# A graph layer's slot table from one product per tile, sums of messages by halves, SiLU and tanh outputs

## The chip, the cores and the metric

One core of a Trainium2 chip. The metric is the time of one execution on the device in microseconds (us); three runs of the kernel before were timed. One more execution was recorded by the hardware profiler, and all rows come from it.

## What is computed

A graph layer over 100,000 nodes with 160 features (64 scalars s and 32 vectors v of three components) and 25,000 edges. Cut to what matters:

```
h = relu(layernorm(x))                                   # every node
w = relu(edge_feature @ W_fc1) @ W_fc2                   # every edge, 224 wide
xs, xv = (s @ W_nl0)[dst], (v @ W_nl1)[dst]              # gathered from h
tp = w0*xs, w3*dot(xv, sh1), w1*xs*sh1, w2*xv, w4*cross(xv, sh1)
agg = segment_sum(tp, src, num_segments=N) / 32
out_s = agg_s @ W_out_s + s @ W_skip0                    # 96 wide
out_v = agg_v @ W_out_v + v @ W_skip1
result = x + concat(silu(out_s[:, :64]), sigmoid(out_s[:, 64:96]) * out_v)
```

## The kernel before

The engines run separate programs that meet at semaphores; nothing is scheduled by a planner. The order on each engine is the order in which the code is written. Loops are unrolled to some depth and closed with a hardware loop. There are three stages.

**Table** (`edge_tiles`, L299). The 25,000 edges are 200 tiles of 125. The nodes are 98 macro tiles of 1,024; eight nodes per partition; a *bin* holds the edges of two of those eight columns (256 nodes), so there are 392 bins with 128 slots each (`CAP`, L53). The stage finds for every edge its slot in its bin and writes a table of which message lies in which slot. Per tile: DVE makes a one-hot of the bin (`bins_of`, L645 to L648, four tiles ahead); PE adds three triangular and full products into running counts (`count`, L1040, called in L1058 to L1065, with `tri_rest`, `ones_bf`, `tri_before`); DVE multiplies the one-hot with the counts and sums (L659), which is the edge's rank; ACT turns the rank into a one-hot of the slot times the tile's number by Abs and Relu (L899, and L892 for the tile before), POOL into a one-hot times the row's number (L496); PE adds both into `p_tile` and `p_row` two tiles later (`table`, L1045 to L1051). At the end PE closes the groups (L1073), ACT copies `p_row` (L908), DVE finds the highest count (L667) and combines both into `slots_i` (L671). If a count exceeds `CAP`, a second, slow form of the nodes stage runs; it is not taken with the reference's inputs.

Ahead of the stage DVE prepares constants (L584 to L643) and the statistics of the first two gathered groups (`stats_e`, L652, L653); behind it DVE prepares edge directions and scales weights (L844 to L860).

**Messages** (`round_e` of each engine; 50 groups of four tiles). POOL gathers node rows, DVE and ACT normalise them, PE turns and multiplies them, DVE forms the products, PE projects them, and SP stores `messages`, 200 numbers per edge with the node's place in column `LOCAL`. Row 0 of `messages` is an empty one. The change leaves this stage alone.

**Nodes** (`round_n` of each engine; 98 macro tiles i). SP loads x three tiles ahead and stores the result. POOL fetches 4 x 128 messages by `slots_i` (L529, `fetch`, two tiles ahead) and raises the variance to the power -1/2 (L535). DVE: the output product of the second half of tile i-1 (`gate`, L757), `shift_n` (L628), `norm_last` (L802), `residual` of i-1 (L772), statistics of i+2 (L610 to L624) with three of the four one-hots of i+1 in its gaps (`hot_n`, L752), `gate` of the first half of i. ACT: sigmoid of both halves (L985), six of the eight normalisations (L958), evacuation of the turned tiles (L965, L966), and the fourth one-hot by Abs and Relu (`distances` L972, `last_hot` L979). PE: transposes (L1176, L1177), the skip products (L1184, L1188) and the sums of the messages (`add`, L1199), in which a one-hot of 128 slots by 128 places multiplies the fetched messages; four products per half tile.

What waits for what around the change: POOL's power waits for DVE's last statistic (L624), DVE's shift for POOL's power, ACT's and DVE's normalisation for the shift, PE's transposes for both. POOL's `fetch` waits for PE's sums four tiles back. In the table stage the rank waits for PE's third count, and PE's next counts for the rank of the tile in front.

## Time and profile before

| what | us |
|---|---|
| timed runs, median (lowest to highest) | 1365.98 (1364.35 to 1367.78) |
| the profiled execution, its own time | 1356.92 |
| its span, first to last instruction | 1355.0 |
| mean granted TensorE clock | 0.984 of full speed |
| busy: PE, DVE, ACT, POOL | 1271.0, 1207.4, 1071.5, 1080.8 |

A row of the profile names the line, the engine, the operation and the tiles written and read. PE is TensorE's matmul, PEld its weight load, DVE VectorE, ACT ScalarE, POOL GpSimd, SP SyncE. The matmuls overlap, so their lengths are longer than the distance at which they start. An instruction's idle time is what its engine stood still ahead of it, with what ended that; "issue" is a wait for nothing that the profile shows. Neighbouring instructions of one group are merged into one row with a count.

### The profile page before, as it was taken

What the parts mean: (1) busy time and instruction counts of PE and PEld (TensorE: products, weight loads), DVE (VectorE), ACT (ScalarE), POOL (GpSimd) and SP (SyncE); (2) the same over time, 40 slices, a digit from 0 to 9 for tenths busy, and PEclk for the clock granted to TensorE, in tenths of its full rate; (3) what the DMA queues carried; (4) which work ended last, traced back from release to release, by engine and by line L of the source; (5) the groups of instructions that cost most, each with busy time, mean ns of one, the idle gap of its engine ahead of it and who ended that gap; (6) DMA issues with size and microseconds to landing.
All of it is one profiled execution on the core that took longest, in us unless ns stands there. A gap on an engine that the chain in (4) does not pass through costs nothing.

```text
span 1355.0 us, 35147 instructions
## 1 busy us (share of the span) xinstructions
PE 1271.0 (94%) x9057; PEld 1142.1 (84%) x9057; DVE 1207.4 (89%) x4348; ACT 1071.5 (79%) x2574; POOL 1080.8 (80%) x1054
## 2 busy tenths in 40 slices
PE   3999979999999999977999999999999999999997
PEld 2777758888888888867899999999999999998996
DVE  6999988888889888856899999999999999999996
ACT  3999977888888888846788788878888888787785
POOL 6999988888878778417788888888888888888883
PEclk9999998999999999988999999999999999999999
DMA  3000003444434444325787887878777787878774
GB/s 109 1 0 0 0 23 83 109 111 113 108 104 118 109 113 108 91 71 140 215 241 227 231 230 230 239 225 240 227 233 228 232 231 233 238 229 234 227 233 128
DMA packets 90918, 212.25 MB, mean 157 GB/s; under 512 B 15030, under 2 KB 56281, under 8 KB 90878
## 3 DMA queue, kind: packets, MB, share of 16 engines
q1 hardware_dynamic: 62462, 155.23, 37.1%
q0 software_dynamic: 28416, 56.56, 17.6%
q8 instruction: 16, 0.26, 0.1%
q14 instruction: 24, 0.20, 0.0%
HBM read 127.73 MB, written 84.00 MB: 156 GB/s over the span
## 4 chain that ended last, share of the span: by engine, by line
PE 50%; POOL 18%; issue 13%; DMA 8%; ACT 5%; DVE 3%; ACTq 0%; POOLq 0%; SPq 0%; DVEq 0%
POOL mg L529 17%; PE bank L1042 7%; DMA mg<-messages,slot_m 7%; PE bank L1105 5%; PE bank L1049 5%; PE bank L1199 5%; PE bank L1184 4%; PE bank L1158 4%; PE bank L1134 3%; PE bank L1122 3%; PE bank L1089 3%; PE bank L1118 2%; PE bank L1120 2%; ACT nn L958 2%; PE bank L1176 2%
## 5 line engine op out<-in xcount | busy, mean ns | idle before, releaser
L529 POOL DMA_INDIRECT mg<-messages,slot_m x392 | 444.8, 1135 | 121.4 <-issue 110.2
L958 ACT ACTIVATE nn<-xb,n_bias,n_rstd 128x160 f32<-128x160 f32 x588 | 300.6, 655 | 22.3 <-DVE n_bias L628 21.4
L1199 PE MATMUL bank<-mg,hot 128*128 128x192 f32 x1568 | 299.2, 334 | 11.6 <-DVE hot L752 11.6
L1184 PE MATMUL bank<-wsk_a,nt_a 128*128 128x160 f32 x1568 | 294.8, 311 | 4.0 <-DVE ob L765 3.0
L1199 PEld LDWEIGHTS bank<-mg,hot 128*128 128x128 f32 x1568 | 251.7, 191 | 11.8 <-DVE hot L752 11.8
L480 POOL DMA_INDIRECT xg<-x,dst_g x200 | 207.4, 1037 | 61.9 <-issue 56.6
L1184 PEld LDWEIGHTS bank<-wsk_a,nt_a 128*128 128x128 f32 x1568 | 226.4, 192 | 13.2 <-issue 9.0
L610 DVE BATCH_NORM_STATS2 n_stat<-xb 128x6 f32<-128x160 f32 x784 | 186.6, 310 | 4.0 <-DMA xb<-x 3.8
L535 POOL TENSOR_TENSOR n_rstd<-n_sum,neg_half 128x8 f32<-128x8 f32 x98 | 163.7, 1671 | 15.4 <-DVE n_sum L624 13.4
L496 POOL TENSOR_SCALAR slot_r<-iota_slot,rank,row_no 125x128 bf16<-125x128 f16 x200 | 160.0, 804 | 6.1 <-DVE rank L659 0.5
L1176 PE MATMUL bank<-ident,nn 128*128 128x128 f32 x784 | 136.0, 296 | 26.1 <-ACT nn L958 21.9
L1176 PEld LDWEIGHTS bank<-ident,nn 128*128 128x128 f32 x784 | 113.3, 207 | 50.1 <-ACT nn L958 43.7
L965 ACT ACTIVATE nt_a<-bank 128x512 f32<-128x512 f32 x196 | 115.7, 590 | 40.7 <-PE bank L1177 38.7
L772 DVE TENSOR_TENSOR ob<-ob,xb 128x1280 f32<-128x1280 f32 x98 | 145.5, 1484 | 0.1
L1188 PE MATMUL bank<-wsk_z,nt_z 128*128 128x64 f32 x784 | 130.1, 248 | 0.0
L1188 PEld LDWEIGHTS bank<-wsk_z,nt_z 128*128 128x128 f32 x784 | 128.5, 191 | 0.0
L882 ACT ACTIVATE hn<-xg,e_bias,e_rstd 125x160 f32<-125x160 f32 x200 | 108.9, 653 | 17.9 <-DVE e_bias L628 17.9
L659 DVE CUSTOM_DVE_ANT_0 rank_junk<-bin_hot,bank 125x392 bf16<-125x392 bf16 x200 | 112.3, 561 | 4.6 <-PE bank L1042 1.4
L918 ACT ACTIVATE tpt<-bank 128x375 f32<-128x375 f32 x200 | 99.5, 497 | 13.1 <-PE bank L1105 11.8
L985 ACT ACTIVATE sg<-bank 128x384 f32<-128x384 f32 x196 | 94.2, 481 | 18.8 <-PE bank L1199 17.3
L752 DVE TENSOR_SCALAR hot<-iota_local,mg 128x256 f32<-128x256 f32 x294 | 93.8, 348 | 16.6 <-DMA mg<-messages,slot_m 16.4
L972 ACT ACTIVATE off<-iota_local,mg 128x256 f32<-128x256 f32 x98 | 49.7, 507 | 74.1 <-DMA mg<-messages,slot_m 74.0
(147 smaller groups left out, 2976.7 us busy)
## 6 DMA issues: line engine op xcount, KB each, us to landing
xb<-x SPq DMA_DIRECT2D x97, 640.0 KB, 6.0
out_dram<-ob SPq DMA_DIRECT2D x97, 640.0 KB, 3.6
messages<-msg SPq DMA_DIRECT2D x50, 390.6 KB
mg<-messages,slot_m POOLq DMA_INDIRECT x392, 5.2
ef<-edge_feat_t SPq DMA_DIRECT2D x50, 125.0 KB, 6.0
xg<-x,dst_g POOLq DMA_INDIRECT x200
xb<-x SPq DMA_DIRECT2D x1, 420.0 KB
out_dram<-ob SPq DMA_DIRECT2D x1, 420.0 KB
```

What stands on the lines that cost most here:

```text
L480: pool.indirect_dma_start(xg[:, b, t, :], None, x[:, :], bass.IndirectOffsetOnAxis(ap=dst_g[:, b, t:t + 1], axis=0)).then_inc(e_x[b], 16)
L496: pool.tensor_scalar(slot_r[:, k % GE, :], iota_slot[0:ET, :], rank[:, k:k + 1], row_no[:, 0:1], ALU.is_equal, ALU.mult).then_inc(b_row, 1)
L529: pool.indirect_dma_start(mg[:, u, k, :], None, messages[:, :], bass.IndirectOffsetOnAxis(ap=slot_m[:, u, k:k + 1], axis=0)).then_inc(n.g[ ...
L535: pool.tensor_tensor(n_rstd[:, u, :], n_sum[:, u, 4, :], neg_half[:, :], ALU.pow).then_inc(n.pw, 1)
L610: last = dve.bn_stats(stat[:, t, :], rows[:, t, :])
L772: dve.tensor_tensor(ob[:, u, :, :], ob[:, u, :, :], xb[:, u, :, :], ALU.add).then_inc(n.res, 1)
L958: last = act.activation(nn[:, u % 2, h, :, g % 4], xb[:, u, g, :], ACT.Relu, bias=n_bias[:, u, g:g + 1], scale=n_rstd[:, u, g:g + 1])
L965: act.activation(nt_a[:, h, :], q_t[h], ACT.Relu)
L1176: pe.transpose(q_t[h][:, t * P:(t + 1) * P], nn[:, u % 2, h, 0:P, t], ident[:])
L1184: pe.matmul(z[:, t, 0:F], nt_a[:, h, t * P:(t + 1) * P], wsk_a[:], start=(t % 2 == 0), stop=False, skip_group_check=True)
L1188: pe.matmul(z[:, 2 * j:2 * j + 2, F:Z], nt_z[:, h, :], wsk_z[:, 2 * V * j:2 * V * j + 2 * V], start=False, stop=every, skip_group_check=True)
L1199: last = pe.matmul(q_z[h][:, t, 0:Z], hot[:, u % 2, g // 2, (g % 2) * P:(g % 2) * P + P], mg[:, u, g // 2, 0:Z], start=False, stop=True, s ...
```

## The change

The table is made by one product per tile. Its slots hold a running number of the message within a block of ten tiles (`row_no` is now 125 k + row, for k = 0 to 9) in one of two tables by turns; how many blocks came before the slot was filled is found by counting, at each block's end, which slots are still empty (`empty`). The bin is now one pair of node columns with 64 slots each (`CAP` 64 for 128 nodes); both counts are kept in one number, with weight 16 for the even and 2^-12 for the odd column, and POOL takes them apart for five tiles at a time. ACT makes the whole slot vector. The counts and tables are f16 instead of bf16. In the nodes stage the one-hot of a bin is 128 x 128, all four on DVE, and each sum is a product over 64 partitions. The output's scalars come from SiLU straight into `ob`, and the gates are tanh(z/2) + 1, with the half in the weights. What is left out is marked by "...": declarations, semaphores, the setup of constants and renamed tiles.

```diff
-    CAP = P
+    CAP = P // 2
+    BR, BLOCK, BATCH = 20, 10, 5
+    W_EVEN, W_ODD, SHARE, ROUND = 2.0 ** 4, 2.0 ** -12, 2.0 ** 16, 1.5 * 2.0 ** 23
+    assert NT % BR == 0 and BR == 2 * BLOCK and BLOCK * ET < 2048 and ET * NT < 2 ** 15
...
-p_tile = bank[1][:, 0:NB]
-p_row = bank[2][:, 0:NB]
+p_tab = [bank[1][:, 0:NB], bank[2][:, 0:NB]]
...
-    def tile_b(t, k):
-        wait(pool, b_tab, t - GE + 1)
-        pool.wait_ge(b_rank, t + 1)
-        pool.sem_inc(s_held, 1)
-        pool.tensor_scalar(slot_r[:, k % GE, :], iota_slot[0:ET, :], rank[:, k:k + 1], row_no[:, 0:1],
-                           ALU.is_equal, ALU.mult).then_inc(b_row, 1)
+    def tile_b(t, k, q):
+        if k % BATCH == BATCH - 1:
+            n, b, first = BR // BATCH * q + k // BATCH, k // BATCH % 2, k - BATCH + 1
+            tiles = bass.ds(t - BATCH + 1, BATCH)
+            ranks = rank[:, first:k + 1]
+            pool.wait_ge(b_rank, t + 1)
+            wait(pool, b_slot, t - BR + 1)
+            pool.tensor_tensor(both[:, b, :], ranks, unit[:, tiles], ALU.mult).then_inc(b_split, 1)
+            pool.tensor_tensor(share[:, b, :], ranks, unit_odd[:, tiles], ALU.mult).then_inc(b_share, 1)
+            pool.wait_ge(b_split, 4 * n + 1)
+            pool.tensor_tensor(evens[:, b, :], both[:, b, :], rounder[:], ALU.add).then_inc(b_split, 1)
+            pool.wait_ge(b_share, 2 * n + 1)
+            pool.tensor_tensor(share[:, b, :], share[:, b, :], first_slot[:, tiles], ALU.add).then_inc(b_share, 1)
+            pool.wait_ge(b_split, 4 * n + 2)
+            pool.tensor_tensor(evens[:, b, :], evens[:, b, :], rounder[:], ALU.subtract).then_inc(b_split, 1)
+            pool.wait_ge(b_split, 4 * n + 3)
+            pool.tensor_tensor(evens[:, b, :], evens[:, b, :], sign[:, tiles], ALU.mult).then_inc(b_split, 1)
+            pool.wait_ge(b_split, 4 * n + 4)
+            pool.wait_ge(b_share, 2 * n + 2)
+            pool.tensor_tensor(slot[:, first:k + 1], evens[:, b, :], share[:, b, :], ALU.add).then_inc(b_dec, 1)
+        if isinstance(t, int) and t == BLOCK:
+            scales(0, 0)
+        if isinstance(t, int) and t == BR - 1:
+            scales(1, 1)
     pool.wait_ge(b_const, 1)
-    scales(0, 0)
-    scales(1, 1)
     edge_tiles(pool, tile_b)
...
+    link(dve.tensor_scalar(weight[:], odd[:], W_ODD - W_EVEN, W_EVEN, ALU.mult, ALU.add))
...
-    dve.memset(most[:], 0.0)
-    dve.tensor_scalar(neg_tile[:], tile_no[:], -1.0, None, ALU.mult).then_inc(b_const, 1)
+    dve.memset(empty[:, 0, :], 0.0)
+    link(dve.memset(empty[:, 1, :], 0.5))
     def bins_of(t, k):
         wait(dve, b_tab, t - BR + 1)
-        dve.tensor_scalar(bin_hot[:, k, :], iota_bin[0:ET, :], bin_of[:, bass.ds(t, 1)], None,
-                          ALU.is_equal).then_inc(b_hot, 1)
+        dve.tensor_scalar(bin_hot[:, k, :], iota_bin[0:ET, :], bin_of[:, bass.ds(t, 1)],
+                          weight[:, bass.ds(t, 1)], ALU.is_equal, ALU.mult).then_inc(b_hot, 1)
     for t in range(4):
         bins_of(t, t)
-    stats_e(0, 0)
-    stats_e(1, 1)
-    shift_e(0, 0)
-    def tile_b(t, k):
+    dve.tensor_scalar(first_slot[:], odd[:], float(CAP), None, ALU.mult)
+    dve.memset(rounder[:], ROUND)
+    dve.tensor_scalar(unit[:], odd[:], 1.0 / W_ODD / W_EVEN - W_EVEN ** -2, W_EVEN ** -2, ALU.mult, ALU.add)
+    dve.tensor_scalar(unit_odd[:], odd[:], SHARE / W_ODD / W_EVEN, None, ALU.mult)
+    dve.tensor_scalar(sign[:], odd[:], -SHARE - 1.0, 1.0, ALU.mult, ALU.add)
+    dve.tensor_copy(row_no[:], row_i[:])
+    link(dve.tensor_copy(unit_of_slot[:], part_i[:]))
+    dve.tensor_scalar(neg_row[:], row_no[:], -1.0, None, ALU.mult).then_inc(b_const, 1)
+    link(dve.tensor_scalar(unit_of_slot[:], unit_of_slot[:], float(CAP), None, ALU.is_ge))
+    link(dve.tensor_scalar(unit_of_slot[:], unit_of_slot[:], 1.0 / W_ODD - 1.0 / W_EVEN, 1.0 / W_EVEN,
+                           ALU.mult, ALU.add))
+    link(dve.tensor_tensor(vec_sq[:], vec[:], vec[:], ALU.mult))
+    link(dve.tensor_tensor(vec_d2[:], vec_sq[:, :, 0], vec_sq[:, :, 1], ALU.add))
+    dve.tensor_tensor(vec_d2[:], vec_d2[:], vec_sq[:, :, 2], ALU.add).then_inc(s_tab, 1)
+    link(dve.tensor_scalar(tmp_a[:], src_i[:], 3, P - 1, ALU.logical_shift_right, ALU.bitwise_and))
+    dve.tensor_copy(place_of[:, :, 0], tmp_a[:])
+    dve.tensor_copy(place_of[:, :, 1], src_i[:])
+    def tile_b(t, k, q):
+        if k % BLOCK == 3 and not (isinstance(t, int) and t < BR):
+            m = 2 * q + k // BLOCK - 2
+            r = k // BLOCK % 2
+            dve.wait_ge(b_tab, t - 13)
+            dve.scalar_tensor_tensor(out=empty[:, r, :], in0=p_tab[r], scalar=0.0, in1=empty[:, r, :],
+                                     op0=ALU.is_equal, op1=ALU.add).then_inc(b_empty, 1)
         wait(dve, b_rank, t - 1)
+        wait(dve, b_dec, BR // BATCH * q + k // BATCH + 1 - BR // BATCH)
         dve.wait_ge(b_pre, t + 1)
         dve.tensor_tensor_reduce(out=rank_junk[:, k % 2, :], in0=bin_hot[:, k, :], in1=p_cnt[k % 2], scale=1.0,
                                  scalar=0.0, op0=ALU.mult, op1=ALU.add,
                                  accum_out=rank[:, k:k + 1]).then_inc(b_rank, 1)
         if tile_exists(t + 4):
             bins_of(t + 4, (k + 4) % BR)
+        if isinstance(t, int) and t == BATCH:
+            stats_e(0, 0)
+        if isinstance(t, int) and t == BLOCK + BATCH:
+            stats_e(1, 1)
+        if isinstance(t, int) and t == BR - 1:
+            shift_e(0, 0)
     edge_tiles(dve, tile_b)
     dve.wait_ge(b_end, 1)
-    dve.reduce_max(most[:], p_cnt[(NT - 1) % 2], AX_X).then_inc(b_most, 1)
-    dve.wait_ge(b_most, 1)
-    dve.tensor_copy(most_i[:], most[:])
+    total = p_cnt[(NT - 1) % 2]
+    link(dve.tensor_scalar(whole[:], total, 1.0 / W_EVEN, ROUND, ALU.mult, ALU.add))
+    link(dve.tensor_scalar(whole[:], whole[:], ROUND, None, ALU.subtract))
+    dve.reduce_max(most[:, 0:1], whole[:], AX_X)
+    link(dve.scalar_tensor_tensor(out=rest[:], in0=total, scalar=1.0 / W_EVEN, in1=whole[:],
+                                  op0=ALU.mult, op1=ALU.subtract))
+    dve.reduce_max(most[:, 1:2], rest[:], AX_X)
     dve.wait_ge(b_rows_sb, 1)
-    dve.scalar_tensor_tensor(out=slots_i[:], in0=p_tile, scalar=float(ET), in1=tab_row[:],
-                             op0=ALU.mult, op1=ALU.add).then_inc(b_fin, 1)
+    for r in range(2):
+        last = dve.scalar_tensor_tensor(out=empty[:, r, :], in0=p_tab[r], scalar=0.0, in1=empty[:, r, :],
+                                        op0=ALU.is_gt, op1=ALU.mult)
+    link(last)
+    dve.tensor_scalar(most[:, 2:3], most[:, 1:2], SHARE, None, ALU.mult)
+    for r in range(2):
+        last = dve.scalar_tensor_tensor(out=tab_row[:, r, :], in0=empty[:, r, :], scalar=2.0 * BLOCK * ET,
+                                        in1=tab_row[:, r, :], op0=ALU.mult, op1=ALU.add)
+    link(last)
+    dve.tensor_tensor(most[:, 3:4], most[:, 0:1], most[:, 2:3], ALU.max)
+    link(dve.tensor_tensor(empty[:, 0, :], tab_row[:, 0, :], tab_row[:, 1, :], ALU.add))
+    dve.tensor_copy(most_i[:], most[:, 3:4])
+    dve.tensor_scalar(slots_i[:], empty[:, 0, :], float(ET * NT), None, ALU.min).then_inc(b_fin, 1)
...
-        def hot_n(i, u, bins=range(BPM - 1)):
+        def hot_n(i, u, bins=range(BPM)):
...
-            dve.tensor_tensor(o[:, :, 0:S], z[:, :, 0:S], sg[:, h, :, 0:S], ALU.mult)
+            dve.tensor_scalar(sg[:, h, :, :], sg[:, h, :, :], 1.0, None, ALU.add).then_inc(n.one, 1)
+            dve.wait_ge(n.fs, 2 * i + h + 1)
+            dve.wait_ge(n.one, 2 * i + h + 1)
             dve.tensor_tensor(o[:, :, S:F].rearrange("p t (i k) -> p t i k", i=3),
                               z[:, :, SG:Z].rearrange("p t (i k) -> p t i k", i=3),
-                              sg[:, h, :, S:SG].unsqueeze(2).to_broadcast((P, 4, 3, V)),
+                              sg[:, h, :, :].unsqueeze(2).to_broadcast((P, 4, 3, V)),
                               ALU.mult).then_inc(n.mul, 1)
...
+    dve.tensor_scalar(wsk_a[:, SG:F], wsk_a[:, SG:F], 0.5, None, ALU.mult)
+    last = dve.tensor_scalar(wsk_z[:], wsk_z[:], 0.5, None, ALU.mult)
...
-    norm_e(0, 0, range(GE))
     act.wait_ge(b_const, 1)
-    def slots_of(t, k):
-        act.activation(slot_t[:, k % GE, :], off_slot[:, k % GE, :], ACT.Relu,
-                       bias=tile_no[:, bass.ds(t, 1)], scale=neg_tile[:, bass.ds(t, 1)]).then_inc(b_slot, 1)
-    def tile_b(t, k):
-        wait(act, b_tab, t - GE + 1)
-        wait(act, b_off, t)
-        act.wait_ge(b_rank, t + 1)
-        act.activation(off_slot[:, k % GE, :], iota_slot[0:ET, :], ACT.Abs, bias=rank[:, k:k + 1],
+    def tile_b(t, k, q):
+        act.wait_ge(b_dec, BR // BATCH * q + k // BATCH + 1)
+        act.activation(off_slot[:, k % 2, :], iota_slot[0:ET, :], ACT.Abs, bias=slot[:, k:k + 1],
                        scale=-1.0).then_inc(b_off, 1)
-        if tile_exists(t - 1):
-            slots_of(t - 1, (k - 1) % BR)
+        wait(act, b_tab, t - BLOCK + 1)
+        act.wait_ge(b_off, t + 1)
+        r = k % BLOCK
+        act.activation(slot_v[:, r, :], off_slot[:, k % 2, :], ACT.Relu, bias=row_no[:, r:r + 1],
+                       scale=neg_row[:, r:r + 1]).then_inc(b_slot, 1)
+        if isinstance(t, int) and t == BR - 1:
+            norm_e(0, 0, range(GE))
     edge_tiles(act, tile_b)
-    act.wait_ge(b_off, NT)
-    slots_of(NT - 1, (NT - 1) % BR)
     act.wait_ge(b_end, 1)
-    act.activation(tab_row[:], p_row, ACT.Copy).then_inc(b_rows_sb, 1)
+    for r in range(2):
+        last = act.activation(tab_row[:, r, :], p_tab[r], ACT.Copy, scale=unit_of_slot[:, 0:1])
+    last.then_inc(b_rows_sb, 1)
...
-        def distances(i, u):
-            act.wait_ge(n.g[u], earlier(i, u, U, 64) + 64)
-            wait(act, n.hot_a, i)
-            act.activation(off[:], iota_local[:], ACT.Abs, bias=mg[:, u, BPM - 1, LOCAL:LOCAL + 1],
-                           scale=-1.0).then_inc(n.off, 1)
-        def last_hot(i, u):
-            wait(act, n.z, 2 * (i - 2) + 2)
-            act.wait_ge(n.off, i + 1)
-            act.activation(hot[:, u % 2, BPM - 1, :], off[:], ACT.Relu, bias=ones[:, 0:1],
-                           scale=-1.0).then_inc(n.hot_a, 1)
-        def sigmoids(i, h):
+        def gates(i, u, h):
+            if h == 0:
+                wait(act, n.st[u], earlier(i, u, U, 16))
             act.wait_ge(n.z, 2 * i + h + 1)
             wait(act, n.mul, 2 * i + h - 1)
-            act.activation(sg[:, h, :, :], q_z[h][:, :, 0:SG], ACT.Sigmoid).then_inc(n.sg, 1)
+            act.activation(sg[:, h, :, :], q_z[h][:, :, S:SG], ACT.Tanh, scale=0.5).then_inc(n.sg, 1)
+            act.activation(ob[:, u, 4 * h:4 * h + 4, 0:S], q_z[h][:, :, 0:S], ACT.Silu).then_inc(n.fs, 1)
...
-                sigmoids(i - 1, 1)
+                gates(i - 1, (u + 3) % U, 1)
             evacuate(i, 1)
             if macro_exists(i + 1):
                 norm(i + 1, (u + 1) % U, 0)
-                if not every:
-                    distances(i + 1, (u + 1) % U)
-            sigmoids(i, 0)
+            gates(i, u, 0)
...
-    def table(t, k):
+    def table(t, k, q):
+        if k % BLOCK == 0:
+            wait(pe, b_empty, 2 * q + k // BLOCK - 1)
         pe.wait_ge(b_slot, t + 1)
-        pe.wait_ge(b_row, t + 1)
-        for o, slot in ((p_tile, slot_t), (p_row, slot_r)):
-            last = pe.matmul(o, slot[:, k % GE, :], bin_hot[:, k, :], start=False, stop=False,
-                             skip_group_check=True)
-        last.then_inc(b_tab, 1)
...
-        if tile_exists(t - 2):
-            table(t - 2, (k - 2) % BR)
+        if tile_exists(t - BLOCK):
+            table(t - BLOCK, (k - BLOCK) % BR, q if k >= BLOCK else q - 1)
     edge_tiles(pe, tile_b)
-    table(NT - 2, (NT - 2) % BR)
-    table(NT - 1, (NT - 1) % BR)
-    for o in (p_cnt[0], p_cnt[1], p_tile, p_row):
-        last = pe.matmul(o, zeros_bf[0:ET, 0:o.shape[0]], zeros_bf[0:ET, :], start=False, stop=True,
+    for t in range(NT - BLOCK, NT):
+        table(t, t % BR, t // BR)
...
-            if h == 0:
-                pe.wait_ge(n.hot, i + 1)
-            else:
-                pe.wait_ge(n.hot_a, i + 1)
-            for t in range(4):
-                g = 4 * h + t
-                last = pe.matmul(q_z[h][:, t, 0:Z], hot[:, u % 2, g // 2, (g % 2) * P:(g % 2) * P + P],
-                                 mg[:, u, g // 2, 0:Z], start=False, stop=True, skip_group_check=True)
+            pe.wait_ge(n.hot, i + 1)
+            for t in (0, 2, 1, 3):
+                slots = slice(CAP * (t // 2), CAP * (t // 2) + CAP)
+                pair = 2 * h + t % 2
+                last = pe.matmul(q_z[h][:, t, 0:Z], hot[slots, u % 2, pair, :], mg[slots, u, pair, 0:Z],
+                                 start=False, stop=True, skip_group_check=True)
             last.then_inc(n.z, 1)
```

## Rows read from the trace of the kernel before

**Rows 1.** Busy time by stage: us; PE, PEld, DVE, ACT, POOL; clock, DMA, GB/s.

```profile
608.00:1332.00 724.00, 688.98 (x4787) 656.37 (x4788) 672.46 (x2400) 582.44 (x1441) 603.82 (x488) 0.99 0.78 226
1332.00:1355.00 23.00, 13.09 (x94) 12.58 (x92) 10.66 (x20) 8.14 (x19) 1.42 (x1) 0.86 0.30 88
```

**Rows 2.** Groups by line, 40 to 160 us: busy us, mean ns, idle before.

```profile
L1042 PE MATMUL bank<-bin_hot,tri_before 125*125 125x392 bf16 x145 | 47.7, 329 | 0.0
```

**Rows 3.** Timeline of DVE and PE at the table's start: start us, us.

```profile
23.84 0.56 DVE L659 CUSTOM_DVE_ANT_0 rank_junk<-bin_hot,bank 125x392 bf16<-125x392 bf16 x1
...
24.32 0.32 DVE L647 TENSOR_SCALAR bin_hot<-iota_bin,bin_of 125x392 bf16<-125x392 f16 x1
...
24.55 0.56 PE L1042 MATMUL bank<-bin_hot,tri_rest 125*125 125x392 bf16 x1 [9.15 <-DVE rank L659]
24.55 0.56 DVE L659 CUSTOM_DVE_ANT_0 rank_junk<-bin_hot,bank 125x392 bf16<-125x392 bf16 x1
...
29.03 0.33 PE L1042 MATMUL bank<-bin_hot,tri_before 125*125 125x392 bf16 x1
...
29.16 0.36 DVE L647 TENSOR_SCALAR bin_hot<-iota_bin,bin_of 125x392 bf16<-125x392 f16 x1
...
29.50 0.56 DVE L659 CUSTOM_DVE_ANT_0 rank_junk<-bin_hot,bank 125x392 bf16<-125x392 bf16 x1
```

**Rows 4.** Timeline of one tile of the nodes stage, POOL and DVE.

```profile
990.47 1.68 POOL L535 TENSOR_TENSOR n_rstd<-n_sum,neg_half 128x8 f32<-128x8 f32 x1
...
993.01 1.49 DVE L772 TENSOR_TENSOR ob<-ob,xb 128x1280 f32<-128x1280 f32 x1
993.65 1.67 POOL L529 DMA_INDIRECT mg<-messages,slot_m  x1 [0.30 <-issue]
...
995.62 0.95 POOL L529 DMA_INDIRECT mg<-messages,slot_m  x1 [0.30 <-issue]
...
997.55 0.16 DVE L624 SCALAR_TENSOR_TENSOR n_sum<-n_sum 128x8 f32<-128x8 f32 x1
...
997.87 1.67 POOL L535 TENSOR_TENSOR n_rstd<-n_sum,neg_half 128x8 f32<-128x8 f32 x1
```

**Rows 5.** Waits of POOL from 608 us on: total us, times, longest.

```profile
POOL n_rstd L535 <- DVE n_sum L624: 7.5, 12, 1.3
```

**Rows 6.** Timeline of DVE ahead of the first rank.

```profile
22.02 1.00 DVE L610 BATCH_NORM_STATS2 e_stat<-xg 125x6 f32<-125x160 f32 x4 [5.29 <-DMA xg<-x,dst_g]
```

**Rows 7.** Groups by line, whole execution: busy us, mean ns, idle before.

```profile
L518 POOL TENSOR_TENSOR cr_a<-w4xv,hat 125x128 f32<-125x128 f32 x50 | 20.6, 411 | 0.0
...
L985 ACT ACT_TABLE_LOAD x1 | 1.3, 1283 | 0.0
...
L600 DVE TENSOR_TENSOR bin_of<-tmp_a,tmp_b 125x200 f32<-125x200 int32 x1 | 0.4, 368 | 0.0
```

**Rows 8.** Timeline of the joint between table and messages, ACT and DVE.

```profile
190.53 0.86 ACT L892 ACTIVATE slot_t<-off_slot,tile_no,neg_tile 125x128 bf16<-125x128 f32 x2
...
192.65 0.50 ACT L908 ACTIVATE tab_row<-bank 128x392 f32<-128x392 f32 x1 [1.26 <-PE bank L1073]
...
193.32 0.56 DVE L671 SCALAR_TENSOR_TENSOR slots_i<-bank,tab_row 128x392 int32<-128x392 f32 x1
...
200.25 1.94 ACT L882 ACTIVATE hn<-xg,e_bias,e_rstd 125x160 f32<-125x160 f32 x4 [3.45 <-DVE e_bias L628]
```

**Rows 9.** Timeline of ACT in the table stage.

```profile
31.02 0.40 ACT L899 ACTIVATE off_slot<-iota_slot,rank 125x128 f32<-125x128 f16 x1
31.33 0.48 ACT L892 ACTIVATE slot_t<-off_slot,tile_no,neg_tile 125x128 bf16<-125x128 f32 x1
31.71 0.39 ACT L899 ACTIVATE off_slot<-iota_slot,rank 125x128 f32<-125x128 f16 x1
```

**Rows 10.** Timeline of ACT at the first tile of the nodes stage.

```profile
615.22 0.51 ACT L972 ACTIVATE off<-iota_local,mg 128x256 f32<-128x256 f32 x1 [13.89 <-DMA mg<-messages,slot_m]
615.76 0.51 ACT L979 ACTIVATE hot<-off,ones 128x256 f32<-128x256 f32 x1
```

135 lines of the change are left out of this document (73 added, 62 removed).

## The prediction

> **What bounds the kernel now.** I read the busy time by stage first: table (24 to 192 us), messages (202 to 596), nodes (608 to 1332). In the nodes stage all four engines are over 80% busy [rows 1], so the share does not say which sets the pace, and I went on to the lines and the waits.
>
> Table stage: 145 tiles in 120 us, 0.83 us each, with five matmuls of 392 columns that start 0.166 us apart, so PE is full [rows 2]. DVE is close behind: rank at 23.84, its bin_hot at 24.32, the next rank at 24.55, that is 0.71 per tile while POOL is not yet making slot_r [rows 3].
>
> Nodes stage: POOL. One tile of 1,024 nodes runs from power to power, 990.47 to 997.87, 7.40 us [rows 4]: 1.68 for the power and 5.72 for four gathers with their issue. From 608 on POOL waits for another engine's n_sum only 12 times, 7.5 us in all [rows 5]. The second gather takes 1.67 us, the third 0.95, because the second meets the residual add on DVE (993.01 to 994.50) [rows 4]. DVE's own loop is almost as long: from the power's end (992.15) it runs shift, norm_last, residual, statistics and hot, and has the next variance at 997.71, 0.16 us ahead of the next power [rows 4]. That is where the 12 waits come from.
>
> **The change, part by part.** The sum is made against the profiled execution, 1356.92 us with a span of 1355.0; the median of the three timed runs is 1365.98, 9.06 higher, and my difference is added to that.
>
> Start of the table stage. Before, rank 0 waits for the second gather's statistics, which begin at 22.02 after 5.29 us of waiting [rows 6]. They now stand at tiles 5 and 15. From 7.04 on DVE has three casts (0.7 us), seven operations on 200 columns (0.25 to 0.37 each [rows 7] for the dearest; 2.1), two memsets of 392 columns (0.8), four bin_hot (0.9), eight small ones (1.5), the vec operations (1.7) and place_of (0.7): estimated by width, rank 0 at 16.0 for 23.84. Gain 7.8 us, between 6 and 9.
>
> Pace. PE falls to four matmuls, 0.66 us. The loop over two tiles is 0.71 (rank 23.84 to tri_rest 24.55) plus two starts of 0.166 plus 0.47 (tri_before 29.03 to rank 29.50) [rows 3], or 0.76 per tile. DVE gives 0.71 plus 0.05, a tenth of a pass over PSUM like slots_i's 0.56 [rows 8], if bin_hot keeps the 0.23 it has with POOL idle. ACT is the largest. It has the same two activations, but before, Relu worked on the tile before, so they overlapped: 0.31 from Abs to Relu, 0.38 from Relu to Abs [rows 9]. Now Relu waits for its own Abs. The trace has that form once: off, 0.51 long, then hot 0.54 after its start [rows 10]. With an Abs of 0.40 this makes 0.43 + 0.39 = 0.82 us per tile, what PE took before. The matmul taken away buys almost nothing; ACT is late next. PE and DVE run ahead until PE stands at the table of ten tiles back.
>
> End of ACT's work. Rank 4 ended at 28.40 (29.50 less two tiles, plus 0.56 [rows 3]), 4.6 us after rank 0, so the first batch is ranked at 20.6. POOL decodes it in seven operations on five columns; 128 columns take 0.41 us [rows 7], and by columns it is far less: estimate 2.0 us with its waits, between 1.0 and 3.5, below the 4.1 of a batch either way, so only the first shows. ACT starts at 22.6, loses 1.9 and 1.8 us to the two statistics on DVE and 1.7 to norm_e (four in 1.94 [rows 8]), and has the last slots at 22.6 + 5.4 + 199 x 0.82 + 0.9 = 192.1, for 191.39 before [rows 8]. The early start is used up by the batch delay and by statistics that used to lie in a wait.
>
> After the last table. From the last slots to the table's copy it is 1.26 us (191.39 to 192.65), now as before. Then slots_i was ready at 193.88 [rows 8]. Now ten passes over 392 columns stand there, most of them a chain on DVE: 0.59 for one that reads PSUM (0.56 and the wait of 0.03), 0.5 for one that doesn't, 0.42 where nothing waits. That is 5.6 us, so 199.0, 5.1 later, with ACT's two copies beside it. ACT's next norm at 200.25 waits for DVE [rows 8], which goes through its whole list first, so all of it counts, with 0.4 for the two scalings of wsk. **Table and joint: +5.5 us**, from +1 (ACT at 0.80) to +10 (at 0.84).
>
> Messages: not touched, only moved. PE at a low clock in a longer joint is covered by DVE's list.
>
> Nodes. Half-high sums on PE, hot of 4 x 128 for 3 x 256 on DVE, off and hot gone from ACT (0.51 each [rows 10]), two shorter activations for one, a product less and a short addition more on DVE: all beside POOL, whose list is the same. Without POOL's cover this would be worth up to 0.7 us per tile on DVE and 1.2 on PE. The residual starts 0.86 us after the power by DVE's own order, so the slow gather stays, and 7.40 with it. What is given is slack: the variance comes 0.3 us sooner. Of the 7.5 us of waits [rows 5] I take 3.5 as gone, with 0 and 7.5 as ends. In the tail (1332 to 1355) PE is busy for 13.09 us [rows 1], and 16 of its 50 starts per tile go to half their time at best, 2.1 us; I take 1.5, between 0 and 2.5. **Nodes: -5 us.**
>
> Sum: +5.5 - 5 = +0.5, so 1366.5 us.
>
> **Rivals.** (a) *Table switches, slower.* There is one ACT_TABLE_LOAD of 1283 ns at the first Sigmoid [rows 7] and none after it. If SiLU and tanh sat in different tables, each half tile would load twice: 5.1 us per tile onto ACT's 5.9 (582.44 over 98 tiles [rows 1]) less 0.7, so 10.3 against 7.4; 98 times that is 290 us, 1656. It decides as soon as ACT passes 7.4. Against it: Relu, Copy and Sigmoid alternate today without a load. Chance 0.03. The Trainium skill, ScalarE: Activation LUTs, "Table sets: the hidden batching unit", says that functions are loaded as named sets, lists tanh with sigmoid and does not place SiLU; by its 2.66 us for every switch the loss would be 10.6 us per tile. The trace agrees on the 1283 ns.
>
> (b) *DVE becomes the bound, slower.* bin_hot gets a second scalar and a multiplication. With POOL at work the next rank came 0.34 after it (29.16 to 29.50 [rows 3]), though PE may have held it. If it stays at 0.34, a tile is 0.48 + 0.34 + 0.05 = 0.87 on DVE; the point from which it decides is 0.82. The table ends 7 us later than in my sum: 1373.5. With 0.43, half the rate, it is 0.96 per tile and 1391. For it: this form is not in the trace. Against: the 0.23 without POOL. Chance 0.20, and 0.05 for ACT at 0.85 or more, at much the same price.
>
> (c) *ACT's wait costs nothing, faster.* With Relu 0.31 after its own Abs, DVE and the two-tile loop set 0.78, and ACT ends 8 us sooner: 1358.5. Against it stands the 0.54 after 0.51 [rows 10]. Chance 0.22.
>
> (d) *The second gather gets free of the residual, faster.* It would take 0.95 for 1.67 [rows 4], but DVE's loop then binds near 7.0: 94 tiles by 0.4, 38 us, 1329. Nothing moves the residual. Chance 0.05.
>
> The fallback, which repeats the nodes stage, would need over 64 edges in a half of 128 nodes; the reference's src gives 55 at most.
>
> **How the numbers follow.** My own case has 0.45, with 1360 to 1372 for its terms. About 0.3% (4.1 us) is what a measurement can tell from no change. Faster by more: (c), (d) and a part of mine, 0.31. Slower by more: (a), (b) and the upper part of mine, 0.29. Same: 0.40. The range reaches from just under (c) to past (b) at 0.87: 1357 to 1379; (a), (d) and the 0.96 of (b) stay outside.
>
> **What would show it.** Rank 0 near 16 us; 0.43 from Abs to Relu and 0.39 from Relu to Abs, 0.82 per tile, PE waiting for slot_v; 5 to 6 us from the table's last matmul to slots_i; powers 7.38 to 7.40 apart with fewer waits for n_sum. I am wrong if the table's tile is under 0.79 or over 0.85 us, if powers are closer than 7.3, or if more than two table loads stand in the nodes stage.

## The result and the profile after

The changed kernel takes **1372.32 us** (median of 9 runs, 1371.11 to 1376.16), the kernel before 1361.37 in as many runs beside it: a ratio of 1.0090, 95% interval 1.0075 to 1.0106. It is slower by 0.9%, where I forecast no change.

The profiled execution took 1375.06 us, with a span of 1373.2. That is 18.2 above the profile of before, but the latter ran 4.4 under its median of these runs and the former 2.7 over, so some 11 us of the 18 are the change. The table below has all 18; one pair of profiles can't say in which rows the other 7 lie. By the stages (start of the profile as zero, starts of the instructions named):

| point | before | after | difference |
|---|---|---|---|
| rank 0 | 23.84 | 16.21 | -7.6 |
| last rank | 189.53 | 188.88 | -0.7 |
| slots_i starts | 193.32 | 204.43 | +11.1 |
| first gather of messages | 608.42 | 620.92 | +12.5 |
| third power | 623.27 | 635.76 | +12.5 |
| last power | 1331.75 | 1350.83 | +19.1 |
| end | 1355.0 | 1373.2 | +18.2 |

One source of the 7 can be seen. The first 20 ranks take 22.99 us here, and 20.3 to 22.6 in e5 to e8 below, which share one chip and have the same table stage; the last rank comes at 186.4 to 189.2 in those four. The profile of after has the longest of all of them.

First, after's VectorE and ScalarE in the middle of the table stage, which answer to [rows 3, 9] (start us, us):

```profile
96.25 0.56 DVE L719 CUSTOM_DVE_ANT_0 rank_junk<-bin_hot,bank 125x392 bf16<-125x392 f16 x1
...
96.74 0.38 DVE L683 TENSOR_SCALAR bin_hot<-iota_bin,bin_of,weight 125x392 f16<-125x392 f16 x1
97.03 0.56 DVE L719 CUSTOM_DVE_ANT_0 rank_junk<-bin_hot,bank 125x392 bf16<-125x392 f16 x1
```

```profile
96.47 0.39 ACT L977 ACTIVATE off_slot<-iota_slot,slot 125x128 f32<-125x128 f16 x1
96.89 0.49 ACT L982 ACTIVATE slot_v<-off_slot,row_no,neg_row 125x128 f16<-125x128 f32 x1
97.29 0.39 ACT L977 ACTIVATE off_slot<-iota_slot,slot 125x128 f32<-125x128 f16 x1
```

ScalarE needs 0.42 + 0.40 = 0.82 us for a tile, as forecast. VectorE gives 0.78, but the pass over `empty` adds 0.47 at every tenth tile and the loop's end 0.17 per twenty: 20 ranks are 16.74 us apart, 0.837 per tile.

Then the joint, for [rows 8]:

```profile
196.54 0.49 ACT L982 ACTIVATE slot_v<-off_slot,row_no,neg_row 125x128 f16<-125x128 f32 x1
198.94 1.07 ACT L990 ACTIVATE tab_row<-bank,unit_of_slot 128x392 f32<-128x392 f32 x2 [1.91 <-PE bank L1138]
...
210.88 0.67 ACT L968 ACTIVATE hn<-xg,e_bias,e_rstd 125x160 f32<-125x160 f32 x1 [2.21 <-DVE e_bias L664]
```

```profile
198.94 0.57 DVE L735 TENSOR_SCALAR whole<-bank 125x392 f32<-125x392 f32 x1 [9.48 <-PE bank L1138]
199.54 0.36 DVE L736 TENSOR_SCALAR whole<-whole 125x392 f32<-125x392 f32 x1
199.94 0.56 DVE L737 TENSOR_REDUCE most<-whole 125x1 f32<-125x392 f32 x1
200.42 0.55 DVE L738 SCALAR_TENSOR_TENSOR rest<-bank,whole 125x392 f32<-125x392 f32 x1
...
201.48 1.03 DVE L743 SCALAR_TENSOR_TENSOR empty<-bank,empty 128x392 f32<-128x392 f32 x2
...
204.43 0.35 DVE L754 TENSOR_SCALAR slots_i<-empty 128x392 int32<-128x392 f32 x1
204.69 1.40 DVE L928 RECIPROCAL vec_r<-vec_r 125x200 f32<-125x200 f32 x1
```

VectorE stands still for 9.48 us ahead of this list and then works through it, with TensorE waiting for its end (5.94 us). Behind slots_i follow another 6.0 us of edge directions and weights (204.69 to 210.69), as in the kernel before, ahead of the shift that ScalarE's normalisation waits for. They read nothing of the table and would fit into the 9.48 us; no run moved them.

Then one tile of the nodes stage, for [rows 4]:

```profile
999.66 1.66 POOL L567 DMA_INDIRECT mg<-messages,slot_m  x1 [0.30 <-issue]
1001.62 0.95 POOL L567 DMA_INDIRECT mg<-messages,slot_m  x1 [0.30 <-issue]
1002.87 1.06 POOL L567 DMA_INDIRECT mg<-messages,slot_m  x1 [0.30 <-issue]
1003.96 1.67 POOL L573 TENSOR_TENSOR n_rstd<-n_sum,neg_half 128x8 f32<-128x8 f32 x1
```

```profile
1002.61 0.48 DVE L834 TENSOR_SCALAR hot<-iota_local,mg 128x128 f32<-128x128 f32 x2
1003.00 0.18 DVE L655 TENSOR_TENSOR n_sum<-n_sum 128x8 f32<-128x8 f32 x1
...
1003.17 0.47 DVE L834 TENSOR_SCALAR hot<-iota_local,mg 128x128 f32<-128x128 f32 x2
1003.56 0.15 DVE L660 SCALAR_TENSOR_TENSOR n_sum<-n_sum 128x8 f32<-128x8 f32 x1
1003.64 0.34 DVE L846 TENSOR_SCALAR sg<-sg 128x128 f32<-128x128 f32 x1
```

and POOL's waits from 620 us on, for [rows 5] (total us, times, longest):

```profile
POOL n_rstd L573 <- DVE n_sum L660: 5.8, 14, 0.8
```

The second gather is as slow as before and the waits are 1.7 us less. But the **fourth gather takes 1.06 us instead of 0.95** [rows 4]: over 94 tiles its mean is 1.040 for 0.953, 8.2 us in all. The first three and the power are unchanged within 0.02 us on average. Powers are 7.48 apart at the median for 7.38; the 95 periods from the third power to the last sum to 715.1 for 708.5, that is 8.2 less 1.7.

### The profile page after: what moved, and what is told of

Read it like the earlier page. It is cut to its first block, busy times and chain, and to the rows that moved or that the text cites. A ratio compares the mean times of both kernels' runs of the same rounds, so it can differ in the third digit from the quotient of the medians.

```text
span 1373.2 us, 34375 instructions
## 1 busy us (share of the span) xinstructions
PE 1213.5 (88%) x8857; PEld 994.9 (72%) x8857; DVE 1207.3 (88%) x4489; ACT 1028.6 (75%) x2576; POOL 982.0 (72%) x1135
## 4 chain that ended last, share of the span: by engine, by line
POOL 39%; PE 32%; issue 17%; DVE 7%; ACT 3%; DMA 1%; DVEq 0%; POOLq 0%; ACTq 0%; SPq 0%
POOL mg L567 30%; POOL n_rstd L573 7%; PE bank L1170 5%; PE bank L1107 4%; PE bank L1223 3%; PE bank L1199 3%; PE bank L1187 3%; PE bank L1154 2%; PE bank L1183 2%; PE bank L1185 2%; DVE rank_junk L719 2%; PE bank L1207 2%; ACT hn L968 2%; PE bank L1115 1%; PE bank L1227 1%
## 5 line engine op out<-in xcount | busy, mean ns | idle before, releaser
L567 POOL DMA_INDIRECT mg<-messages,slot_m x392 | 453.6, 1157 | 120.9 <-issue 109.8
L1263 PE MATMUL bank<-mg,hot 64*128 64x192 f32 x1568 | 181.2, 350 | 12.6 <-DVE hot L834 12.6
L1241 PE MATMUL bank<-ident,nn 128*128 128x128 f32 x784 | 147.0, 310 | 24.3 <-ACT nn L1041 18.1
L1241 PEld LDWEIGHTS bank<-ident,nn 128*128 128x128 f32 x784 | 109.9, 209 | 80.8 <-issue 43.5
L1263 PEld LDWEIGHTS bank<-mg,hot 64*128 64x128 f32 x1568 | 123.2, 186 | 25.9 <-DVE hot L834 12.7
L849 DVE TENSOR_TENSOR ob<-bank,sg 128x384 f32<-128x384 f32 x196 | 109.3, 558 | 20.4
L719 DVE CUSTOM_DVE_ANT_0 rank_junk<-bin_hot,bank 125x392 bf16<-125x392 f16 x200 | 111.6, 558 | 4.2 <-PE bank L1107 3.5
L834 DVE TENSOR_SCALAR hot<-iota_local,mg 128x128 f32<-128x128 f32 x392 | 93.6, 283 | 15.8 <-DMA mg<-messages,slot_m 15.7
L1170 PE MATMUL bank<-ident,tp 125*128 125x125 f32 x600 | 103.3, 281 | 3.8 <-DVE tp L790 3.2
L982 ACT ACTIVATE slot_v<-off_slot,row_no,neg_row 125x128 f16<-125x128 f32 x200 | 98.6, 493 | 8.7 <-PE bank L1115 0.4
```

Source lines behind the costliest of these rows:

```text
L567: pool.indirect_dma_start(mg[:, u, k, :], None, messages[:, :], bass.IndirectOffsetOnAxis(ap=slot_m[:, u, k:k + 1], axis=0)).then_inc(n.g[ ...
L719: dve.tensor_tensor_reduce(out=rank_junk[:, k % 2, :], in0=bin_hot[:, k, :], in1=p_cnt[k % 2], scale=1.0, scalar=0.0, op0=ALU.mult, op1=AL ...
L1170: last = pe.transpose(p_tt[:, i * ET:(i + 1) * ET], tp[:, c, t, TURN[i]:TURN[i] + P], idt)
L1241: pe.transpose(q_t[h][:, t * P:(t + 1) * P], nn[:, u % 2, h, 0:P, t], ident[:])
L1263: last = pe.matmul(q_z[h][:, t, 0:Z], hot[slots, u % 2, pair, :], mg[slots, u, pair, 0:Z], start=False, stop=True, skip_group_check=True)
```

## The experiments

They ran in four jobs on four chips: e1 to e4, e5 to e8, e9 to e11, and e12. The kernel before took 1433, 1434, 1360 and 1434 us on them. It was profiled on one chip only, but the variants show where the 74 us lie: mostly in the messages stage, which no edit touches. Between its first and last group (ScalarE's `hid`) there are 382 to 384 us in before, after, e9, e10 and e11 and 442 to 453 in the others; TensorE is busy for 199.3 us from 330 to 530 us in after and for 176.8 in e8, which is the same kernel. The nodes stage of e8 is 5.5 us longer than that of after, nearly all in its first tiles. The cause was not looked for. So ratios are against the kernel before in the same job, and microseconds are read from the stages. The diffs show the core of each edit; removed originals, waits and renamed tiles are left out.

**e8, the changed kernel again**, unaltered. 

> The changed kernel itself, unaltered, on the same chip as the three others, so that they can be set against it. Both theories: 7.48 us between powers, fourth gather 1.05 us, 16.7 us per 20 ranks, and the ratio to the kernel before as first measured, 1.0075 to 1.0106.

Measured: ratio 1.0069 (1.0042 to 1.0096), just under the range expected; powers 7.48 apart, fourth gather 1.042 on average. The loss and its places come back on another chip.

**e2, Relu on the tile before.**

```diff
 act.activation(off_slot[:, k, :], iota_slot[0:ET, :], ACT.Abs, bias=slot[:, k:k + 1], ...)
+if tile_exists(t - 1):
+    slots_of(t - 1, (k - 1) % BR)
```

> The changed kernel with ScalarE's Relu of the table stage working on the tile before (20 off_slot tiles instead of 2), as in the kernel before; nothing else. Theory A (VectorE sets the table's pace: 0.78 per tile, plus 0.47 at every tenth tile for the pass over empty and 0.17 per loop of 20, 16.74 us per 20 ranks; ScalarE at 0.82 only trails it): 20 ranks stay at 16.7 to 16.8 us, Abs and Relu need about 0.70 per tile when they have work, and only the end of ScalarE's work comes sooner, by 2 to 3 us; the time falls by 2 to 4 us. Rival B (my prediction: ScalarE's wait for its own Abs sets the pace at 0.82): 20 ranks fall to 15.3 to 15.6 us and the time by 8 us or more.

Measured: ratio 1.0067 (1.0042 to 1.0091). ScalarE's rows:

```profile
96.55 0.39 ACT L984 ACTIVATE off_slot<-iota_slot,slot 125x128 f32<-125x128 f16 x1
96.84 0.48 ACT L979 ACTIVATE slot_v<-off_slot,row_no,neg_row 125x128 f16<-125x128 f32 x1
97.22 0.39 ACT L984 ACTIVATE off_slot<-iota_slot,slot 125x128 f32<-125x128 f16 x1
97.52 0.48 ACT L979 ACTIVATE slot_v<-off_slot,row_no,neg_row 125x128 f16<-125x128 f32 x1
98.41 0.40 ACT L984 ACTIVATE off_slot<-iota_slot,slot 125x128 f32<-125x128 f16 x1 [0.42 <-POOL slot L533]
```

It works at 0.68 per tile and then waits for POOL's decoding of ranks that aren't there yet. 20 ranks still take 16.72 to 16.73 us, so ScalarE does not set the pace (theory A). Its last vector starts at 193.10, 5.4 us behind the last rank, for 7.65 in e1 on the same chip, and slots_i comes 2.3 us sooner. In the whole time the gain is too small to be told: e1 has 1.0084 (1.0057 to 1.0110).

**e3, bin_hot without the weight.** The multiplication is left out, and the odd part of the final test of the counts with it, so slots and fetched rows are others than in the reference; only the table stage is read.

```diff
-weight[:, bass.ds(t, 1)], ALU.is_equal, ALU.mult).then_inc(b_hot, 1)
+None, ALU.is_equal).then_inc(b_hot, 1)
```

> The changed kernel with a bin_hot without the multiplication by weight (the second scalar operand is left out, so the counts of odd and even columns run together and the table's slots are wrong; the test of the counts against the capacity is left without its odd part too). Theory A (the next rank comes 0.30 us after bin_hot instead of 0.23 because of the second scalar and operation): the distance falls to 0.23, VectorE would need 15.3 us per 20 tiles, and then ScalarE's 0.82 binds at 16.4 to 16.5 us per 20 ranks; the stage ends 2 to 3 us sooner. Rival B (the distance has another cause, such as f16 for bf16 or a wait for PE): it stays at 0.30 and so does the pace of 16.74.

```profile
96.40 0.32 DVE L683 TENSOR_SCALAR bin_hot<-iota_bin,bin_of 125x392 f16<-125x392 f16 x1
96.63 0.56 DVE L719 CUSTOM_DVE_ANT_0 rank_junk<-bin_hot,bank 125x392 bf16<-125x392 f16 x1
```

The next rank comes 0.23 us behind bin_hot, and from the 40th to the 160th tile 20 ranks take 16.40 to 16.42 us, which is ScalarE's 20 x 0.82. Both halves of theory A hold: the weight costs 0.07 us per tile, and ScalarE is the next bound, 2% behind. The end of the stage moved less than expected: the last rank comes 3.3 us sooner than in e1, slots_i 1.7 (2 to 3 expected), since ScalarE's lag is kept. The whole took 1.0843 times as long, with powers 8.8 apart on average. VectorE waits there for loads of x 45 times, 77.4 us in all from 720 to 1320 us, for 7 times and 3.1 us in after. That the other rows which the wrong slots fetch cause this is likely, and was not tested.

**e4, statistics ahead of the first rank.**

```diff
 dve.tensor_copy(place_of[:, :, 1], src_i[:])
+stats_e(0, 0)
+stats_e(1, 1)
+shift_e(0, 0)
```

> The changed kernel with the statistics of the first two gathered groups (and their powers and normalisation) put back ahead of the first rank, as in the kernel before; nothing else. Theory A (the early start is nearly all given back, because the statistics cost 6.2 us of the first 20 ranks, 23.0 for 16.74 us, once they stand between ranks): rank 0 moves from 16.2 to 23.5 to 24.5 us, 20 ranks from the first on take 17 to 18 us instead of 23.0, and the table ends 1 to 3 us later; time +1 to +3 us. Rival B (the term of 7.8 us that I counted for the start is kept to the end): table and time 7 to 8 us later.

Measured: ratio 1.0103 (1.0079 to 1.0126); rank 0 at 24.69, 20 ranks 17.1 us, last rank 3.6 us behind that of e1 on the same chip. So of 8.4 us of a sooner start 3.6 arrive at the end. Nearer to A, a little above its 3. The number is a rough one: with the same table code, the last rank of e5 to e8 varies by 2.7 us on one chip.

**e11, the end of the table.** e2's edit, and the counts' groups closed ahead of the last ten table products, so that VectorE's passes for the highest count fall into its wait:

```diff
+for o in p_cnt:
+    last = pe.matmul(o, ..., start=False, stop=True, ...)
+last.then_inc(b_most, 1)
 for t in range(NT - BLOCK, NT):
     table(t, t % BR, t // BR)
```

> The changed kernel with two edits at the end of the table stage: Relu on the tile before (as in e2, which brought slots_i forward by 2.3 us), and the counts' groups closed right behind the last rank, so that VectorE's passes for the highest count (whole, rest, two maxima, 2.5 us) lie in its idle time there and not behind the last table product; the table's copies are signalled one by one. Theory (those passes stand on the chain from the last slot vector to slots_i, 7.9 us long): that chain falls to 5.0 to 5.8 us, slots_i is ready 4.4 to 5.2 us sooner than in the changed kernel and the time falls by 3 to 5 us. Rival (the copies of the two tables bound that chain, the passes being beside them): chain stays over 7 us and the gain is the 2.3 us of e2 alone.

```profile
191.23 0.56 DVE L740 TENSOR_REDUCE most<-rest 125x1 f32<-125x392 f32 x1
195.41 1.04 DVE L743 SCALAR_TENSOR_TENSOR empty<-bank,empty 128x392 f32<-128x392 f32 x2 [3.62 <-ACT tab_row L995]
...
198.43 0.35 DVE L754 TENSOR_SCALAR slots_i<-empty 128x392 int32<-128x392 f32 x1
```

Last slot vector 193.06, slots_i 198.43: 5.4 us for 7.9. slots_i is 5.2 to 5.3 us sooner than in e9 and e10 of the same job, which keep the old end. Ratio 1.0042 (1.0026 to 1.0059), for 1.0090 of the changed kernel on another chip and 1.0079 of e9, which keeps the old end, in this job: about half of the loss is this chain with ScalarE's lag ahead of it.

**e1, the addition of 1 on ScalarE.** In after, the fourth gather was about 0.95 long in all 11 tiles in which the short addition on sg did not lie beside it, so I took that for the cause. (In four more tiles it lay beside it and the gather took 0.95 to 1.02 all the same.)

```diff
-dve.tensor_scalar(sg[:, h, :, :], sg[:, h, :, :], 1.0, None, ALU.add).then_inc(n.one, 1)
+act.activation(sg[:, h, :, :], sg[:, h, :, :], ACT.Relu, bias=ones[:, 0:1]).then_inc(n.one, 1)
```

> The changed kernel with the addition of 1 to the gates taken from VectorE and made by ScalarE (Relu of tanh plus one, which is never negative); nothing else. Theory A (in the changed kernel the fourth gather of a nodes tile takes 1.06 us instead of 0.95 because VectorE's short addition on sg lies beside it; in the 14 of 94 tiles where it does not, the gather takes 0.95): the fourth gather falls back to 0.95 us in nearly all tiles, the median distance of two powers from 7.48 to 7.38 us, and the whole by 8 us or a little more (0.6%) against the changed kernel. Rival B (the four narrower one-hots of 128 x 128 are what slows it): fourth gather stays at 1.06, powers 7.48 apart, time within 2 us of the changed kernel. Rival C (ScalarE's two extra activations of about 0.3 us hold up the evacuation): powers further apart than 7.48 and the time above the changed kernel.

```profile
1002.77 1.06 POOL L567 DMA_INDIRECT mg<-messages,slot_m  x1 [0.30 <-issue]
```

Measured: ratio 1.0084 (1.0057 to 1.0110). The addition is gone and the gather takes 1.06 as before (mean 1.049). Theory A fell: the two had only come together.

**e5, the fourth one-hot on ScalarE**, as before the change.

```diff
-for b in (range(0, 2), range(2, BPM))]
+for b in (range(0, 2), range(2, BPM - 1))]
...
+distances(i + 1, (u + 1) % U)
...
+last_hot(i + 1, (u + 1) % U)
```

> The changed kernel with the fourth one-hot of a nodes tile (128 x 128) back on ScalarE by Abs and Relu, as in the kernel before; VectorE makes three, two in the first gap of the statistics and one in the second. With the addition of 1 taken away from VectorE the fourth gather still took 1.05 to 1.06 us, so that addition is not its cause. Theory B (the second narrow one-hot in the second gap, which starts 0.47 us behind the gather's start, lengthens it): the fourth gather falls to 0.95 us, two powers are 7.38 us apart instead of 7.48, and the time is 8 to 10 us under the changed kernel. Rival D (narrow one-hots as such, or a shift of the whole list by a few tenths of a microsecond against the gather): the gather stays at 1.05.

Measured: ratio 1.0079 (1.0048 to 1.0109); fourth gather 1.043 on average, powers 7.48 apart. Theory B fell too.

**e6, all one-hots behind the variance.**

```diff
-stats_n(i + 2, (u + 2) % U, hots)
+stats_n(i + 2, (u + 2) % U)
+if macro_exists(i + 1) and not every:
+    hot_n(i + 1, (u + 1) % U)
```

> The changed kernel with all four one-hots of a nodes tile made behind the variance instead of in the gaps of the statistics (VectorE's order alone). Theory B (one-hots beside the fourth gather lengthen it by 0.1 us): only statistics lie beside it, it takes 0.95, the variance comes some 0.7 us sooner, POOL's 14 waits for it (5.8 us) go, and powers are 7.36 to 7.38 apart: 9 to 14 us under the changed kernel. Rival E (the one-hots now lie beside the power and lengthen that, or PE waits for them): the power takes more than 1.67 us or PE's wait for hot grows to more than 50 us, and the time does not fall.

```profile
1003.78 1.95 POOL L567 DMA_INDIRECT mg<-messages,slot_m  x1 [0.30 <-issue]
...
1007.28 0.95 POOL L567 DMA_INDIRECT mg<-messages,slot_m  x1 [0.30 <-issue]
```

```profile
1003.44 1.47 DVE L856 TENSOR_TENSOR ob<-ob,xb 128x1280 f32<-128x1280 f32 x1
...
1007.61 0.95 DVE L834 TENSOR_SCALAR hot<-iota_local,mg 128x128 f32<-128x128 f32 x4
```

Measured: ratio 1.0096 (1.0071 to 1.0120). Here three or four one-hots lie beside the fourth gather, and it takes 0.95 in every tile: they do not slow it. But in about half of the tiles the residual starts 0.3 us later, and the second gather takes 1.95 there (1.80 on average). In after, before and here it ends 0.82 us behind the residual's end (1004.91 to 1005.73 here, 994.50 to 995.32 in [rows 4]): it seems to stand still from about 0.1 us behind its start until the residual is done. Neither of my two theories gave this; powers went to 7.64.

**e9, three one-hots in the first gap and one in the second**, to shift the list by one.

```diff
-for b in (range(0, 2), range(2, BPM))]
+for b in (range(0, 3), range(3, BPM))]
```

> The changed kernel with three one-hots in the first gap of the statistics and one in the second, instead of two and two (VectorE's order alone; the same instructions). So far the fourth gather took 1.05 us wherever the product of two sums (n_sum from n_sum, two operands in SBUF) started 0.10 to 0.14 us behind the gather's start, with or without the addition of 1, with three or four one-hots; and 0.95 where it started elsewhere, even with four one-hots beside it. Theory P (it is where VectorE's list lies against the gather's start): the product now starts 0.30 us behind the gather's start, the gather takes 0.95 to 1.0, and powers are 7.38 to 7.43 apart, 5 to 9 us less than the changed kernel. Rival D (narrow one-hots as such): it stays at 1.05 and powers at 7.48.

```profile
1005.62 1.02 POOL L567 DMA_INDIRECT mg<-messages,slot_m  x1 [0.30 <-issue]
```

Measured: ratio 1.0079 (1.0060 to 1.0098); fourth gather 1.016 on average, powers 7.45 apart, nodes stage 710.2 us for 714.3 in e11 of the same job. The same instructions in another order give back 4 us, partly in the gather (a third of its lengthening), partly in POOL's waits for the variance. It is a matter of where the list lies against the gather's start, though 1.02 is above what I expected. The tiles of all fourteen traces, ordered by the start of the product of two sums (L655 in after) behind the fourth gather's start, say the same:

| product starts behind the gather | fourth gathers | their mean |
|---|---|---|
| -0.20 to 0.05 us | 99 | 0.950 |
| 0.10 to 0.14 | 594 | 1.055 |
| 0.15 to 0.27 | 101 | 0.951 |
| 0.28 to 0.36 | 96 | 1.020 |
| 0.38 to 1.1 | 182 | 0.952 |

Before the change it stood at 0.25 to 0.27 in most tiles, after it at 0.10 to 0.13: a shift of VectorE's list by some 0.14 us made the 8.2 us. Whether the product itself meets the gather or a neighbour that moves with it is left open. That it has two operands in SBUF is not enough: in e6 the last operation of the variance, which has two as well and is as short, starts 0.10 to 0.14 us behind 83 of the fourth gathers, and they take 0.95.

**e7 and e10, the residual in halves.** One half follows each gate; in e7 the second half's gate comes ahead of the shift, in e10 behind it. Both have e1's edit.

```diff
 if macro_exists(i + 1):
     shift_n(i + 1, (u + 1) % U)
+if macro_exists(i - 1):
+    gate(i - 1, (u + 3) % U, 1)
+    residual(i - 1, (u + 3) % U, 1)
...
 gate(i, u, 0)
+residual(i, u, 0)
```

> The changed kernel with the addition of 1 on ScalarE, and VectorE's residual (128 x 1280, two operands in SBUF) cut in two of 640: the first half right behind the first half's gate, beside POOL's power, the second behind the shift. Theory F (the second gather takes 1.65 instead of 0.95 us because the residual lies 0.8 us beside it; no other operation of VectorE does that): the second gather falls to 0.95 to 1.0, the first rises from 1.02 to 1.3 at most, POOL's list is 6.8 to 7.1 us long, and VectorE's own list of about 7.0 us sets the distance of powers: 7.0 to 7.25, 20 to 45 us under the changed kernel. Rival G (the half beside the first gather lengthens it by all that the second gains, up to 0.7 us): powers 7.4 to 7.5 apart and no gain. Rival H (VectorE's list is longer than POOL's by now): powers over 7.5 apart, slower, with POOL waiting for n_sum in every tile.

> As e7 (addition of 1 on ScalarE, residual in two halves), but VectorE's shift comes ahead of the second half's gate, and the second half of the residual behind that gate. In e7 all four gathers took 0.95 to 1.03 us, but the shift waited for a gate that waits for ScalarE, whose work starts from the shift, and powers were 8.27 us apart. Theory F (that loop was all that was wrong): gathers stay at 0.95 to 1.03, POOL's list is 6.75 to 6.9 us, powers are 6.8 to 7.1 apart, and the time is 35 to 60 us under the changed kernel. Rival G (the second half now lies beside the second gather's start and lengthens it): second gather over 1.3 and powers over 7.2. Rival K (PE or the loads of x, at 0.79 of the DMA engines' time now, become the bound): gathers short, POOL waits for n_sum, powers 7.1 to 7.4.

e10: ratio **0.9901** (0.9880 to 0.9922), 1345.83 us, faster than the kernel before in the same job, and 24.5 us under e9, which stands for the changed kernel there. Theory F had expected 35 to 60.

```profile
1001.85 1.66 POOL L573 TENSOR_TENSOR n_rstd<-n_sum,neg_half 128x8 f32<-128x8 f32 x1 [0.42 <-DVE n_sum L660]
1003.70 1.02 POOL L567 DMA_INDIRECT mg<-messages,slot_m  x1 [0.19 <-issue]
1006.01 0.94 POOL L567 DMA_INDIRECT mg<-messages,slot_m  x1 [1.29 <-issue]
1007.26 0.95 POOL L567 DMA_INDIRECT mg<-messages,slot_m  x1 [0.30 <-issue]
```

```profile
1002.26 0.82 DVE L855 TENSOR_TENSOR ob<-ob,xb 128x640 f32<-128x640 f32 x1
1003.54 0.17 DVE L664 SCALAR_TENSOR_TENSOR n_bias<-n_sum,n_rstd 128x8 f32<-128x8 f32 x1 [0.46 <-POOL n_rstd L573]
1003.67 0.56 DVE L846 TENSOR_TENSOR ob<-bank,sg 128x384 f32<-128x384 f32 x1
1004.26 0.82 DVE L855 TENSOR_TENSOR ob<-ob,xb 128x640 f32<-128x640 f32 x1
```

One half lies beside the power. The other starts 0.56 us behind the first gather's start and ends at 1005.08; in most tiles that is 0.04 to 0.06 us behind the start of the second gather, which in the tile shown comes late. The four gathers take 1.02, 0.95, 0.95 and 0.95 on average, powers are 7.08 apart at the median (7.24 on average) and the nodes stage is 26.6 us shorter than in e11 of the same job. POOL now waits about 0.6 us per tile for the variance, which is rival K's part, and three times over 1 us ahead of a gather, for which the trace names no one.

All traces together bear theory F out, and show its condition. Where the residual or a half of it was under way when a gather started and ended 0.2 us or more behind that start, 1049 of 1056 gathers ended 0.80 to 0.85 us behind its end. Where it ended within 0.12 us of the start (177 gathers), none was longer than without it. Where it started 0.15 us or more behind the gather's start (1289 gathers), all but two were as short as without it, though it lay beside them.

e7: ratio 1.0444 (1.0417 to 1.0472). Its gathers were short too (0.95 to 1.03), but after ten tiles powers settled 8.27 apart, as rival H has it: POOL waits for n_sum in most tiles (66 times from 720 to 1320 us, 105.4 us in all). Its stages (us; PE, PEld, DVE, ACT, POOL busy; granted clock, DMA, GB/s):

```profile
735.30:742.20 6.90, 5.90 (x48) 5.44 (x48) 6.37 (x26) 4.82 (x15) 5.60 (x5) 1.00 0.84 248
...
900.00:1000.00 100.00, 85.00 (x605) 76.17 (x606) 78.39 (x301) 70.10 (x207) 67.50 (x61) 0.91 0.73 208
```

and where TensorE first stood still:

```profile
745.41 0.75 PE L1246 MATMUL bank<-ident,nn 128*128 128x128 f32 x4 [2.70 <-ACT nn L1044]
```

The tile at 735 took 6.90 us. Then TensorE waited 2.70 us for ScalarE's normalisation, and from 720 us on the trace has 65 such waits, 1.7 us each on average. Four skip products take 1.27 us at 1000.02 and 0.71 at 1004.59: with a granted clock of 0.91 on average, TensorE ran part of the time at its lower level of 1.2 GHz.

**e12, e10 and e11 together**, with the second pair of one-hots behind the variance.

```diff
-stats_n(i + 2, (u + 2) % U, hots)
+stats_n(i + 2, (u + 2) % U, (hots[0], None))
+if hots[1]:
+    hots[1]()
```

> The edits of e10 and e11 in one kernel, and VectorE's second pair of one-hots moved behind the variance. In e10 the powers were 7.08 us apart in the quiet tiles: 1.66 for the power, then 5.3 from VectorE's shift to its next variance, after which VectorE has 0.46 us of idle time ahead of the next shift; POOL waited 0.4 to 0.6 us per tile for that variance. Theory (that loop sets the distance): the variance comes 0.4 us sooner, POOL's own list of 6.7 us becomes the bound, powers are 6.75 to 6.9 apart at the median, and with the 5 to 6 us of the table's end the time is 25 to 45 us under e10's ratio of 0.990, a ratio to the kernel before of 0.957 to 0.972. Rival (the longer waits that about every third tile of e10 had, 7.3 to 7.6 us, come from elsewhere, such as the issue of the gathers, and grow): mean distance stays at 7.2 and only the table's 5 to 6 us are gained, ratio 0.985 to 0.988.

```profile
1000.00:1100.00 100.00, 86.50 (x620) 77.63 (x618) 81.97 (x313) 70.49 (x208) 67.40 (x62) 0.91 0.73 211
```

```profile
1004.09 0.94 PE L1256 MATMUL bank<-ident,nn 128*128 128x128 f32 x4 [1.80 <-ACT nn L1050]
```

Measured: ratio 1.0367 (1.0334 to 1.0399), slower than all but e7 and e3, where I expected 0.957 to 0.972. The table's end was as in e11 (slots_i at 198.08). Six single periods are 6.83 to 6.94 us, what the theory gave, but most are 8.0 to 8.3, the same pattern as e7: TensorE waits, its granted clock falls to 0.91 to 0.95, and the chain from normalisation to gate grows. Both ran on chips on which the kernel before took 1434 us, e10 on one with 1360. Whether the pattern comes with VectorE's order or with the chip was not settled, since e10 and e12 were not run on the same one. For the chip speaks that on those with 1434 the untouched messages stage runs longer too, with TensorE waiting for ScalarE, whatever the kernel. So e10's gain is shown for one chip.

## Why the prediction was right or wrong

**Start of the table.** Rank 0 forecast at 16.0, measured 16.21. Right in size, with some luck: the terms that I listed add up to 15.4 (7.04 and 8.4), not to 16.0. That most of it would be used up was right too: in e4 3.6 of 8.4 us are left at the end, give or take the spread named there.

**Pace.** The time per tile was close (0.82 forecast, 0.837 measured), the engine was wrong. I let VectorE have 0.76 with "if bin_hot keeps the 0.23 it has with POOL idle" and named 0.34 as rival (b). It is 0.29 to 0.30, with POOL idle as well (between the first two ranks of after, 16.21 and 16.99, bin_hot starts at 16.70), and e3 puts the whole 0.07 down to the second operand and operation. Rival (b) was thus half true, and its point of decision, 0.82, was passed by 0.02. e2 shows that ScalarE's wait on its own Abs, on which my sum rested, costs only at the end.

**End of ScalarE's work.** Forecast 192.1, measured 197.03, the largest error of the table stage: +4.9. The first twenty tiles lost 1.8 us more than my 5.4; tiles 20 to 180 took 132.7 us for 131.2; and in the last twenty, whose code is laid out apart from the loop, a tile took 0.88 and not 0.82:

```profile
185.23 0.39 ACT L977 ACTIVATE off_slot<-iota_slot,slot 125x128 f32<-125x128 f16 x1
185.71 0.49 ACT L982 ACTIVATE slot_v<-off_slot,row_no,neg_row 125x128 f16<-125x128 f32 x1
```

that is 1.2 us more, and one pause of 0.3 us in addition. The chain behind it was forecast at 6.9 and took 7.75, of which 0.65 is TensorE's closing of the groups (1.91 for 1.26 us): its products stood 0.88 apart by then and took 0.51 each; in e11, where they came 0.68 apart, one took 0.34. The granted clock of after, in its rows by stage, with the columns of [rows 1]:

```profile
189.00:197.40 8.40, 4.57 (x15) 1.27 (x14) 0.45 (x2) 6.90 (x18) 5.90 (x12) 0.71 0.14 40
197.40:213.00 15.60, 5.97 (x21) 3.24 (x20) 13.06 (x43) 4.32 (x10) 3.31 (x5) 0.50 0.10 29
```

I had priced the closing at the full clock; TensorE, waiting for ScalarE, had already come down to 1.2 GHz. Table and joint were +5.5 in the forecast, with +1 and +10 as bounds, and +10.9 in the profile (end of slots_i): just over the upper bound.

**Messages** were "only moved". They cost 1.9 us more within their first seven groups. No experiment was made on that.

**Nodes.** The period was to stay at 7.40 with fewer waits. The slow gather did stay, the waits fell by 1.7 for 3.5, the tail by 0.9 for 1.5. The step that failed is the one that read "all beside POOL, whose list is the same": POOL's list has the same instructions, but their lengths hang on what VectorE does beside them, and I had used this rule myself for the second gather without asking it of the fourth, against which the change shifts VectorE's list. It cost 8.2 us, +6.6 with the waits, for -3.5. What the change takes from the others is real and hidden: the sums of a half tile take 0.92 us for 1.52, and TensorE is busy for 1213.5 us in all for 1271.0.

The range, 1357 to 1379, held the time, and the time itself was 5.8 us over my 1366.5. A part of that is luck: I added my difference to 1365.98, the median of three runs, and with nine the kernel before has 1361.37. The sum of +0.5 was 10 us too low for the measured +11. In the profiles two terms are off in the same direction: table and joint by 5.4 us, nodes by 10.7, most of it the fourth gather. Together they are more than the 10, since the profiles lie 7 us further apart than the medians.

## What to carry to other kernels

When an engine's list is the bound and "stays the same", compare also what the other engines do beside each of its instructions, above all beside its start; a reordering there can be worth more than the work removed elsewhere (e10, on its one chip: 26.6 us from order and a cut in two, against nothing from 57 us less of TensorE). A faster per-item form that needs a longer closing chain should have that chain sorted by what waits for it: here 2.5 us of bookkeeping for a branch that is read at the very end stood in front of everything. And an order can give short periods for some tiles and then settle at longer ones (e7: 6.8 to 7.7 with one of 8.8, then 8.27 from the eleventh on): look at the sequence of periods, not at one.

## What the runs showed of the hardware

A gather by POOL is held up by VectorE's residual, an addition with two operands in SBUF, if that is under way about 0.13 us behind the gather's start, and then until the residual ends: 1.67 us with 0.85 us of it left at the gather's start, 1.95 with 1.13, 0.95 without. One that ends by then or starts later costs nothing. The Trainium skill, SBUF — State Buffer, "Who interferes with whom", says that such an operation contends with a GpSimd instruction that reads SBUF; these rows agree. The same section says that a tensor_scalar in a two-port mode locks GpSimd out altogether, for which the f32 one-hots would be candidates; in e6 up to four of them lie beside a gather of 0.95 us, so no row here shows that.

The fourth gather takes 0.1 us more where the product of two sums of 8 columns starts 0.10 to 0.14 us behind its start, and 0.07 more at 0.28 to 0.36; which operation holds it is open.

A second scalar operand with its operation lengthens VectorE's 392 columns from 0.23 to 0.30 us between starts. And two activations in a row that depend on each other start 0.42 us apart inside the hardware loop and 0.48 outside of it, where both waits are on constants; in the first ten tiles, which lie outside too but have one wait less, it is 0.42.
